# Attention and mixture-of-experts layer on one Trainium2 core: new places in the written-out order of the expert stage

## What is computed

```
x: (4, 512, 256), four batches of 512 tokens
mod = silu(c) @ wmod -> sa, ca, ga, sb, cb, gb per batch
h = layernorm(x) * (1 + ca) + sa
x = x + ga * attention(h)                       # 16 heads of 128, causal
h = layernorm(x) * (1 + cb) + sb
d = h @ down_w + down_b                         # 256 -> 128
probs = softmax(h @ router_w + router_b - cost); top 2 of 8; gate = softmax of the two
out = sum_k gate_k * sum_e expert_e(d * [e is chosen])     # hidden sizes 128 to 512, gelu
out = out + 0.1 * shared(d)
x = x + gb * (out @ up_w + up_b + gelu(h) @ core_w + core_b)
```

## Time and profile before

| | before |
|---|---|
| median of 3 runs | 822.38 us |
| the profiled execution | 828.41 us |
| its span (first to last instruction) | 826.3 us |
| TensorE busy | 794.3 us (96%) |
| VectorE busy | 680.8 us (82%) |
| ScalarE busy | 628.8 us (76%) |
| GpSimd busy | 439.7 us (53%) |

### The profile page before, as it was taken

How to read it: one execution, slowest core, us unless ns; L and a number is a source line. 1 busy time by engine, 2 the same in 40 slices (tenths; PEclk the granted TensorE clock), 3 DMA queues, 4 the chain that set the end, 5 groups by cost and what they waited for, 6 DMA issues and landing times.

```text
span 826.3 us, 14461 instructions
## 1 busy us (share of the span) xinstructions
PE 794.3 (96%) x4806; PEld 710.6 (86%) x4806; DVE 680.8 (82%) x1649; ACT 628.8 (76%) x1417; POOL 439.7 (53%) x305
## 2 busy tenths in 40 slices
PE   8899899999999999999999999999999898999897
PEld 7689888999999999999999999999988676777686
DVE  4789898888888888888888878889898987797766
ACT  3787878778878888778887788887779586675864
POOL 2555355654555556544566544575453474667544
PEclk8999999999999999999999999999999899999999
DMA  7253233343223433233233442244232141111131
GB/s 247 75 168 72 57 88 91 92 112 73 64 68 81 111 107 90 68 85 73 64 91 90 103 109 64 64 110 115 66 74 54 46 129 34 53 43 66 64 97 58
DMA packets 47593, 70.54 MB, mean 85 GB/s; under 512 B 5536, under 2 KB 38464, under 8 KB 47392
## 3 DMA queue, kind: packets, MB, share of 16 engines
q1 hardware_dynamic: 47008, 68.81, 31.7%
q0 software_dynamic: 368, 0.81, 0.3%
q10 hardware_dynamic: 144, 0.00, 0.0%
HBM read 25.49 MB, written 2.17 MB: 33 GB/s over the span
## 4 chain that ended last, share of the span: by engine, by line
PE 69%; ACT 16%; DVE 10%; issue 4%; DMA 1%; SPq 0%; DVEq 0%; ACTq 0%
PE M L729 10%; PE M L730 10%; PE M L728 10%; PE T L728 7%; PE T L729 7%; PE T L730 7%; PE S L728 5%; PE S L730 5%; PE S L729 5%; ACT PB L620 3%; ACT PB L669 3%; DVE S L1136 2%; ACT pth L696 2%; ACT qk L682 1%; DVE Gr L1294 1%
## 5 line engine op out<-in xcount | busy, mean ns | idle before, releaser
L620 ACT ACTIVATE PB<-S,nb 128x128 f32<-128x128 f32 (+3 forms) x256 | 133.9, 533 | 109.3 <-DVE nb L1136 109.3
L570 POOL TENSOR_TENSOR X<-X,fb 128x512 f32<-128x512 f32 x64 | 83.0, 1298 | 245.6 <-DVE fb L1173 245.6
L577 POOL TENSOR_TENSOR ptl<-ptl,pth 128x640 fp32r<-128x640 f32 x126 | 195.8, 1576 | 32.0 <-ACT pth L696 32.0
L669 ACT ACTIVATE PB<-PB,ri 128x256 f32<-128x256 f32 (+3 forms) x256 | 124.5, 581 | 6.8 <-DVE ri L1145 6.7
L1136 DVE CUSTOM_DVE_ANT_0 S<-S,cc 128x128 f32<-128x128 f32 (+3 forms) x256 | 117.5, 522 | 1.3 <-PE S L730 1.3
L1121 DVE TENSOR_TENSOR qk<-M,qk 128x512 fp32r<-128x512 f32 x108 | 74.6, 690 | 45.2 <-ACT qk L682 45.2
L1152 DVE STREAM_TRANSPOSE gab<-PB 128x256 f32<-128x256 f32 (+2 forms) x192 | 109.3, 622 | 0.0
L728 PE MATMUL S<-qk 128*128 128x128 f32 (+3 forms) x256 | 86.8, 339 | 4.7 <-DVE qk L1121 4.7
L728 PE MATMUL M<-hh,W 128*128 128x512 f32 x222 | 87.3, 393 | 0.7 <-DVE hl L1107 0.7
L696 ACT CAST pth<-ptl 128x640 fp32r<-128x640 f32 x128 | 87.9, 746 | 0.1
L730 PE MATMUL M<-hh,W 128*128 128x512 f32 x222 | 87.2, 393 | 0.0
(11 more groups left out here) (255 smaller groups left out, 2444.9 us busy)
## 6 DMA issues: line engine op xcount, KB each, us to landing
ptl<-gab SPq DMA_DIRECT2D x256, 160.0 KB, 3.1
stage<-in_wat SPq DMA_DIRECT2D x16, 512.0 KB, 5.0
gab<-scw SPq DMA_DIRECT2D x16, 256.0 KB, 3.3
tmp<-scw SPq DMA_DIRECT2D x16, 256.0 KB, 3.6
X<-in_x SPq DMA_DIRECT2D x3, 512.0 KB, 8.6
stage<-in_wfa SPq DMA_DIRECT2D x3, 512.0 KB, 4.8
out<-X SPq DMA_DIRECT2D x3, 512.0 KB, 2.9
X<-in_wmod SPq DMA_DIRECT2D x1, 1024.0 KB, 11.7
```

The lines of the kernel that those rows point to most:

```text
L570: pool.tensor_tensor(X[:, a:a + 512], X[:, a:a + 512], fb[:, c2 * 512:c2 * 512 + 512], ALU.add).then_inc(s_y, 1)
L577: pool.tensor_tensor(ptl[u % 2][:, s], ptl[u % 2][:, s].bitcast(F32), pth[u % 2][:, s].bitcast(F32), ALU.subtract).then_inc(s_pl, 1)
L620: ins = act.activation(PB[:, P_OFF[i]:P_OFF[i] + w], PS[bk][:, a:a + w], ACT.Exp, bias=nb[:, i:i + 1], scale=-1.0, accum_out=sm[:, i:i + 1])
L669: act.activation(p, p, ACT.Copy, scale=ri[:, i:i + 1]).then_inc(s_P3, 1)
```

## The change

All of it is in the order of the list, with one group of three VectorE instructions moved besides. No product, buffer or engine changes.

- Steps 3 to 9 of batch 0's router go from chunks 0:0 to 0:2 into the end of the attention, ahead of VectorE's part of `dn` 0. Steps 10 to 14 go from 0:4 and 0:5 to 0:0 and 0:1, its `wt` from 0:7 to 0:3, the last `pt` from 0:5 to 0:3, the last `z` from 0:7 to 0:6, the last two `wo` from 0:9 and 0:10 to 0:8 and 0:9, `wh` 21 and 22 one and two chunks earlier.
- The three instructions that clear `wgw` and `Dm` go from behind the low part of `z` 61 to ahead of step 10 of batch 0.
- Layernorm of batches 2 and 3: `nm` 6 in 0:10 and 0:11 (was 0:9, 0:10), `nm` 7 in 0:19 and 0:20 (was 0:18, 0:19), each at least a chunk behind its `nb`.
- Batch 1: steps 3 to 7 in 0:11 and 0:12 (were 0:12 and 0:13), `wt` in 0:19 (was 1:1); `dta` one chunk earlier for two of its three parts, `dt` in 1:0 (was 1:1).
- Batch 2: `r` in 1:5 (was 1:7), `wt` in 2:0 (was 2:2). Batch 3: `r` in 2:4 (was 2:1), steps 3 to 14 in 2:14 to 2:19 (were 2:8 to 2:13), `wt` in 3:0 (was 3:2).
- `gx` 0 in 1:7 and 1:9 (was 1:8, 1:10), its `hs` as much earlier; the second `gx` of batches 1, 2 and 3 one chunk later. `o` 0 in 1:6 (was 1:7). `up` of batches 1 and 2 in chunks 7 and 8 (were 8 and 10), of batch 0 in 1:11 and 1:12 (was 1:11 and 1:13). `xb` of batches 1 and 2 in chunk 0 of the next batch (was 19), of batch 3 in 3:16 (was 3:18).

```diff
--- before.py
+++ after.py
@@ -105,7 +105,8 @@
         plan += post.get(i, [])
     u = NU - 1
     plan += [("S", u), ("wo", u // 2 - 2, 1), ("v", u // 2, 1), ("ex", u), ("ri", u), ("r", 0), ("rs", 0, 1),
-             ("rs", 0, 2), ("pt", u - 1), ("ra",), ("wx", u // 2 - 2, 1), ("b1",), ("dn", 0), ("z", u - 2)]
+             ("rs", 0, 2), ("pt", u - 1), ("ra",), ("wx", u // 2 - 2, 1), ("b1",)] + [("rs", 0, k) for k in range(3, 10)] + [
+             ("dn", 0), ("z", u - 2)]
     return plan + [("norm", u), ("ty", u), ("tr", u), ("z", u - 1), ("ld", 22)]
 
 
@@ -117,57 +118,60 @@
     def put(t, j, *events):
         at.setdefault((t, j), []).extend(events)
 
-    put(0, 0, ("rs", 0, 3), ("rs", 0, 4), ("rs", 0, 5))
-    put(0, 1, ("wo", last - 1, 0), ("rs", 0, 6), ("rs", 0, 7))
-    put(0, 2, ("wo", last - 1, 1), ("rs", 0, 8), ("rs", 0, 9))
-    put(0, 3, ("wh", 21))
-    put(0, 4, ("rs", 0, 10), ("rs", 0, 11), ("rs", 0, 12))
-    put(0, 5, ("rs", 0, 13), ("rs", 0, 14), ("pt", NU - 1))
-    put(0, 6, ("wh", 22))
-    put(0, 7, ("wt", 0), ("wl", 0), ("wl", 1), ("wl", 2), ("z", NU - 1), ("st", 6, 0), ("st", 6, 1))
-    put(0, 8, ("st", 6, 2), ("st", 6, 3))
-    put(0, 9, ("wo", last, 0), ("nb", 6), ("nm", 6, 0))
-    put(0, 10, ("wo", last, 1), ("wl", 3), ("nm", 6, 1))
-    put(0, 11, ("d0", 0))
+    def router(b, steps, weights):
+
+        first, exps, rest = steps
+        put(*first, ("r", b))
+        put(first[0], first[1] + 1, ("rs", b, 1), ("rs", b, 2))
+        for c in range(4):
+            put(exps[0], exps[1] + c, ("rp", b, c))
+        for k, j in enumerate(rest[1], 3):
+            put(rest[0], j, ("rs", b, k))
+        put(*weights, ("wt", b))
+
+    put(0, 0, ("rs", 0, 10), ("rs", 0, 11), ("rs", 0, 12))
+    put(0, 1, ("wo", last - 1, 0), ("rs", 0, 13), ("rs", 0, 14))
+    put(0, 2, ("wo", last - 1, 1), ("wh", 21))
+    put(0, 3, ("pt", NU - 1), ("wt", 0), ("wl", 0), ("wl", 1), ("wl", 2))
+    put(0, 4, ("wh", 22))
+    router(1, ((0, 5), (0, 7), (0, (11, 11, 11, 12, 12, 14, 14, 16, 16, 16, 17, 17))), (0, 19))
+    put(0, 6, ("z", NU - 1))
+    put(0, 7, ("st", 6, 0), ("st", 6, 1))
+    put(0, 8, ("wo", last, 0), ("st", 6, 2), ("st", 6, 3))
+    put(0, 9, ("wo", last, 1), ("wl", 3), ("nb", 6))
+    put(0, 10, ("nm", 6, 0))
+    put(0, 11, ("nm", 6, 1), ("d0", 0))
     put(0, 12, ("d0", 1))
-    put(0, 13, ("dn", 1), ("d0", 2))
-    put(0, 14, ("h2", 2, 0))
-    put(0, 16, ("h2", 2, 1))
-    for k, j in enumerate((15, 16, 16, 17)):
-        put(0, j, ("st", 7, k))
-    put(0, 18, ("nb", 7), ("nm", 7, 0), ("dta", 0))
-    put(0, 19, ("nm", 7, 1), ("dta", 1))
-    put(0, 20, ("dta", 2))
-    put(1, 1, ("dt",), ("xb", 0))
-    put(1, 2, ("h2", 3, 0))
-    put(1, 4, ("h2", 3, 1))
-    put(1, 5, ("D", 0))
-    put(1, 6, ("hs", 0, 0))
-    put(1, 8, ("gx", 0, 0), ("hs", 0, 1))
-    put(1, 10, ("gx", 0, 1))
-    for b, n in ((1, 5), (2, 28), (3, 43)):
-        def at_(i, *events):
-            put(*divmod(i, NC + 1), *events)
-        at_(n, ("r", b))
-        at_(n + 1, ("rs", b, 1), ("rs", b, 2))
-        for c in range(4):
-            at_(n + 2 + c, ("rp", b, c))
-        for k, m in enumerate((7, 7, 7, 8, 8, 9, 9, 11, 11, 11, 12, 12), 3):
-            at_(n + m, ("rs", b, k))
-        at_((22, 44, 65)[b - 1], ("wt", b))
+    put(0, 13, ("dn", 1))
+    put(0, 14, ("h2", 2, 0), ("d0", 2))
+    put(0, 15, ("h2", 2, 1), ("st", 7, 0))
+    put(0, 16, ("st", 7, 1), ("st", 7, 2))
+    put(0, 17, ("st", 7, 3), ("dta", 0))
+    put(0, 18, ("nb", 7), ("dta", 1))
+    put(0, 19, ("nm", 7, 0), ("dta", 2))
+    put(0, 20, ("nm", 7, 1))
+    put(1, 0, ("dt",))
+    put(1, 3, ("h2", 3, 0))
+    put(1, 4, ("h2", 3, 1), ("D", 0))
+    put(1, 5, ("hs", 0, 0))
+    put(1, 7, ("gx", 0, 0), ("hs", 0, 1))
+    put(1, 9, ("gx", 0, 1))
+    late = 14, 14, 14, 15, 15, 16, 16, 18, 18, 18, 19, 19
+    router(2, ((1, 5), (1, 8), (1, late)), (2, 0))
+    router(3, ((2, 4), (2, 5), (2, late)), (3, 0))
     for t in range(1, B):
-        late = 3 * (t == 1)
+        first = t == 1
+        put(t, 0, ("xb", t - 1))
         put(t, 3, ("D", t))
-        put(t, 6 + late // 3, ("o", t - 1))
-        put(t, 8 + late, ("up", t - 1, 0))
-        put(t, 9 + late, ("hs", t, 0))
-        put(t, 10 + late, ("up", t - 1, 1))
-        put(t, 11 + late, ("gx", t, 0), ("hs", t, 1))
-        put(t, 13 + late, ("gx", t, 1))
+        put(t, 6, ("o", t - 1))
+        put(t, 11 if first else 7, ("up", t - 1, 0))
+        put(t, 12 if first else 8, ("up", t - 1, 1))
+        put(t, 12 if first else 9, ("hs", t, 0))
+        put(t, 14 if first else 11, ("gx", t, 0), ("hs", t, 1))
+        put(t, 17 if first else 14, ("gx", t, 1))
         if t + 1 < B:
             put(t, 17, ("dn", t + 1))
-            put(t, 19, ("xb", t))
-    put(B - 1, 18, ("xb", B - 1))
+    put(B - 1, 16, ("xb", B - 1))
     chunks = B * (NC + 1)
     plan, later = [], []
     for n in range(chunks + LAG + 1):
@@ -1119,10 +1123,6 @@
                         hi, lo = zs(ev[1])
                     src = bank(ev)[:].rearrange("p (s n) -> p s n", s=2) if kind == "z" else bank(ev)[:]
                     v.tensor_tensor(lo, src, hi.bitcast(F32), ALU.subtract).then_inc(me, 1)
-                    if ev == ("z", NU - 3):
-                        v.tensor_scalar(wgw[:, 0:384], cc[:, 0:384], 0.0, None, ALU.mult)
-                        v.tensor_scalar(Dm[:], cc[0:96, 0:128], 0.0, None, ALU.mult)
-                        link(v.tensor_copy(wgw[:, 384:512], ident))
                 elif kind == "S":
                     u = ev[1]
                     if u > 0:
@@ -1175,6 +1175,10 @@
                                     ALU.mult).then_inc(me, 1)
                 elif kind in ("r", "rs"):
                     b, k = ev[1], (0 if kind == "r" else ev[2])
+                    if (b, k) == (0, 10):
+                        v.tensor_scalar(wgw[:, 0:384], cc[:, 0:384], 0.0, None, ALU.mult)
+                        v.tensor_scalar(Dm[:], cc[0:96, 0:128], 0.0, None, ALU.mult)
+                        link(v.tensor_copy(wgw[:, 384:512], ident))
                     if k:
                         v.wait_ge(s_rt, 15 * b + k)
                     router(ev, b, k).then_inc(s_rt, 1)
```

## The result

The kernel after takes **819.08 us** (median of 12 executions, 817.11 to 820.94), the kernel before 824.17 on the same chip (12 executions, 819.92 to 828.21): a ratio of 0.9935, with a 95% interval of 0.9915 to 0.9956. A second measurement on another chip gave 819.37 against 822.83, 0.9954 (0.9930 to 0.9978). The change gains 3.5 to 5.1 us where 9.3 were forecast, and about 3.4 when all executions of both kernels are put together. The direction was right, the size was not.

The account below looks back on a forecast made before the run. TensorE's order was the bound, with 26.8 of the stage's 188.6 us lost to waits and slow clock. After, 12.7 of waits and 4.8 for three falls make 17.5, so 9.3 less: 822.4 to 813.1 us, range 808.3 to 820.3.

Parts of the forecast that it names:

- sum after: Whole expert stage: waits and small rests left after the change, 12.7 us, plus three clock falls, 4.8, make 17.5.
- the median of before lies 6.0 lower; I take the same difference from it: Final time: the 9.3 us gained on the profiled execution, 828.4, is taken from the median 822.4, giving 813.1.
- I take 1.6 us for one fall: Expert stage: each drop of TensorE's clock to 1.2 GHz costs 1.6 us, half of 3.4 less a little hidden.
- the sum of TensorE's idle time in 0:11 to 1:4 as before: Sign of being wrong, late batch 0 to early batch 1: TensorE's total idle time there stays unchanged.
- `wt` 0 in 0:3: Batch 0: TensorE waits 2.65 us for VectorE's step 14, held by GpSimd's first `wo` addition.
- 0:11 to 1:4 ... 4.9: Late batch 0 to early batch 1: 4.9 us of waits plus one clock fall, for 7.2 lost before.
- `gx` 0: 1:5 to 1:13: wait of 0.6 us for 1.82, no clock fall, since GpSimd's powers do not hold VectorE.
- 1:14 to 2:16: Late batch 1 through most of batch 2: 2.4 us of waits plus one clock fall, for 6.5 lost before.
- (b): Rival, stretches holding a `wt`: the wait only moves, 3.7 us less, 818.7 us; 22 in 100.
- (a): Rival, whole stage: the clock does not fall, 14.1 us less, 808.3 us; 12 in 100.
- (c): Rival, 2:16 and 3:16: the expert sums stay late, gain 6.9 us, 815.5 us; 12 in 100.
- (d): Rival, the four `wt`: they become the bound, waits double, six falls, 3.5 us slower, 825.9 us; 9 in 100.

Follow-up runs that it names:

- e7: Kernel after with `wt` 0 in 0:5, the last `z` in 0:8 and the last two `wo` in 0:10 and 0:11: 815.36 us, ratio to before 0.9913.
- e8: e7 with `wt` 1 in 1:0 and `wt` 2 in 2:1, one chunk later each: 815.47 us, ratio to before 0.9905.
- e11: e8 with `dn` 2 in 1:15 and not in 1:17: 815.95 us, ratio to before 0.9907.
- e1: Kernel before, unchanged, measured once more: 821.99 us, ratio to before 1.0006.
- e0: Kernel after, unchanged, measured once more on another chip: 819.37 us, ratio to before 0.9954.
- e6: Kernel after with `nm` 7 a chunk sooner, back in 0:18 and 0:19: 822.64 us, ratio to before 0.9999.
- e5: Kernel after with `xb` of batches 1 and 2 back in chunk 19: 825.50 us, ratio to before 1.0037.
- e2: Kernel after with `wt` 0 in 0:5 and not in 0:3: 821.76 us, ratio to before 0.9988.
- e9: Kernel after with the second `gx` of batch 1 back in 1:16: 820.73 us, ratio to before 0.9972.
- e10: Kernel after with the second `h2` transpose of batch 2 back in 0:16 from 0:15: 821.63 us, ratio to before 0.9982.
- e4: Kernel before with only the batch 0 part (router, `wt` 0, last `pt`, `z`, `wo`, `wh`, clearing): 825.88 us, ratio to before 1.0033.
- e12: Kernel after with the batch 0 part undone, all else of the change kept: 819.48 us, ratio to before 0.9951.

## Why the prediction was right in its direction and wrong in its size

**The larger step that failed: the "sum after", 12.7 with "small rests of 0.1 at seven places" for 0.7 of it, was set against 26.8.** The 26.8 of before is what is left of the stage's length when the needs are taken off, so it holds every loss, named or not. The 12.7 of after is built up from waits that I could name. Of the 9.3 that came out, 5.6 were waits (18.3, which is 26.8 less 8.5 for the clock, to 12.7) and 3.7 clock (8.5 to 4.8). Counted alike, the named waits in the stage go from 15.3 to 12.8, 2.5 less and not 5.6, and TensorE's idle time goes down by 2.6. The rest is in both kernels: after, at full clock, loses 18.1, and 18.1 - 12.8 = 5.3 of it stand in no row of these views. With the same needs e7, e8 and e11, which have no fall in the stage either, leave 5.4, 5.6 and 6.5. The prediction left 0.7 of this to the kernel after.

That the profiled execution came out at 819.17 where 819.1 was forecast is luck. The waits and rests were 5.4 too low (12.7 for 18.1), and three falls for 4.8 did not come in that execution: 17.5 for 18.1.

**The second step: "the median of before lies 6.0 lower; I take the same difference from it".** A median execution has less clock to give back than one with 17 us at half clock in the stage. Twice (1 - mean clock) times the span is the time at half clock: 33 us in the profiled execution of before, 18.5 in the mean of the 96, 12.3 in that of after's 22. How much of the 18.5 lies in the stage can only be estimated: with 3.4 to 13.6 in the first 100 us (e1) and some 2 in the last microseconds, 3 to 13 and not 17. Profile against profile, the clock is 6.1 of the 8.7 us of stage. Over all executions, 0.0038 of mean clock at 510 to 600 us is 1.9 to 2.3 us. At equal clock (0.989 to 0.991) 42 executions of before have a median of 822.0 and 7 of after 819.5; one step higher (0.992 to 0.994) it is 820.4 and 818.7: 1.7 to 2.5 that are not clock, and 1.5 by one common slope for all 118. Together that is about the 3.4 that all executions show. The second profiles of the two programs say much the same: e1's stage has 13.6 us at half clock and takes 185.9, e0's has 10.2 and takes 182.8, some 3 less. The right sum would have been some 2 for waits and 2 for the clock, from 822.4 to about 818.5. Putting only this second step right would have left 5.6 + 2 = 7.6, far from what was measured. That the clock itself gains is plausible by the waits that went, but that it gains in after because of them is only argued: e0 shows that the same waits may come with or without a fall.

**"I take 1.6 us for one fall":** 1.0 to 1.25 by the slopes of e1, and 1.2 between the profiles of before and after (6.1 us for 17.1 at half clock), with single pairs at 1.0 and 2.7.

**The prediction's own sign of being wrong came true:** "the sum of TensorE's idle time in 0:11 to 1:4 as before". It was 4.83 us (34.19 less 29.36 busy) and is 4.68 (33.52 less 28.84). Of the signs of being right, 1:5 starts at 696.7 and 2:17 at 763.4, as said, and no `dt` or `D` waits; but `wt` 1 waits 1.21 and not some 3, and the slow clock of the stage is 0 in after's first profile and 10.2 us in e0's, where about 10 was said.

**The waits after, place by place:** the total of the named ones is near (12.8 in the stage; 12.0 without the small rests), but not the terms.

- `wt` 0 in 0:3: 2.65 forecast, 2.70 measured, and its cause is as told. The timeline of all engines:

```profile
644.32 1.26 POOL L574 TENSOR_TENSOR X<-X,fb 128x512 f32<-128x512 f32 x1 [6.54 <-DVE fb L1173]
...
644.48 1.15 DVE L1015 TENSOR_TENSOR wg<-rt 128x32 f32<-128x32 f32 x1
```

The `wg` step that takes 0.19 in batch 2 takes 1.15 under GpSimd's addition. "`pt` 63 leaves GpSimd 0.4 before `z` wants it" came down to 0.1 (652.6 to 652.7), since GpSimd's second addition took 2.21 us and not 1.3. Of the gap between 4.3 lost here and 3.4, 0.6 is in the needs: `z` takes 1.96 of TensorE (652.74 to 654.70) and not 1.4. "A fall of the clock" here came in e0's profile and not in after's.

- "0:11 to 1:4 ... 4.9": 6.5 lost. The late sum in 0:16 (1.4 forecast) did not come, nor did the 3.2 at `wt` 1 (1.21) or the 0.3 at `dt`. The walk left out the banks: `h2` of batch 2 in 0:15 takes the bank of `dn` 1's product and waits 1.31 for its low part, `dta` waits 1.46 for the low part of `h2` itself, and two more waits for banks take 0.70 in 1:4 and, just behind this stretch, 0.41 in 1:5. I had followed VectorE's queue with TensorE's main operands and not with the tiles that `h2`, `dta` and `dn` pass on. One backlog of VectorE, met at other doors: 4.7 us of waits where 4.9 were forecast, at other places and as long as before.

- `nm` 7: "no longer blocks ScalarE for 5.07 us", right; the idle time before it is 1.90 us in after, and TensorE doesn't meet it. e6 shows what it is worth.

- `gx` 0: 0.6 forecast by rows, 1.4 by the rule of the Trainium skill that the prediction names, 0.72 measured. The timeline of all engines shows why:

```profile
708.92 0.81 DVE L1291 TENSOR_TENSOR gxl<-stage,gxh 128x512 fp32r<-128x512 f32 x1
709.13 2.10 POOL L556 TENSOR_TENSOR rt<-ebase,rt 128x8 f32<-128x8 f32 x1
```

VectorE's subtraction with two SBUF inputs ends 1.5 us before GpSimd's power does. The power doesn't hold it. It had begun 0.21 us before the power, but in the earlier trace rows the same instruction begins inside a power and takes 0.69 us all the same. The Trainium skill (GPSIMD Engine Reference, Specifications) has the SBUF interfaces contended by any VectorE instruction with two SBUF inputs; here the trace agrees for GpSimd's additions (1.15 us for the `wg` step above) and not for its powers.

- 1:14 to 2:16: 2.4 of waits and a fall forecast, 5.0 lost, no fall. `up` waits 0.38 and 0.39 (0.5 forecast). `wt` 2 waits 1.20 (1.9), `D` not at all. Left out: **the first product of batch 2 needs the low part of `dn` 2**, and that stands on VectorE behind the held `gx` 1. Timeline of all engines:

```profile
728.39 1.27 POOL L547 TENSOR_TENSOR stage<-stage,prod 128x512 f32<-128x512 f32 x1
728.46 1.74 DVE L1291 TENSOR_TENSOR gxl<-stage,gxh 128x512 fp32r<-128x512 f32 x1
...
730.13 0.68 DVE L1284 TENSOR_TENSOR ur<-M,ur 128x512 fp32r<-128x512 f32 x1
```

The prediction had "perhaps a hold ahead of the steps" and charged it to `wt` 2 alone; TensorE met it sooner, with 2.09 us at 2:0's first product.

- `xb`: "2.1 us of hold gone", right and undersold: e5 puts the place of `xb` at about 6 us, since both `wt` that moved sooner hang on it.

**The rivals.** (b), *the wait only moves*, at 818.7, came nearest, and its reason holds for much of the stage: e2, e9, e10 and e11 each took away a wait and found most of it a few chunks later, and e8 found one of its two. It said no change in the three stretches with a `wt`; in fact the large waits went and others came, and some 2 us stayed gone. The other argument in it, that the busiest engine leaves an order nothing to win, doesn't hold: TensorE is 96% busy in e7 too, which is 4 us faster than after. (a), no fall at all, is what after's profile shows, but at 819.2 and not at 808.3: the rests that the sum left out stand in the place of the falls. (c) did not come; the sums wait 0.2. (d) did not come for after, but e5 shows that its mechanism is real: held in these very steps, `wt` costs more than the change gains.

**What stays open.** How often a wait of 1.5 to 3 us brings a fall is known only from the few profiled executions (e0); over all executions only the mean clock of the whole span stands here. What the 5.3 us of unnamed rest consist of was not looked into. Which parts of the change bring the gain on top of before was tested, e4 and e12 aside, by undoing single steps; the new places of batch 3's router, of `up`, of `o` and of `gx` 0 were not undone. Nor was it tried whether a lighter VectorE queue in 0:12 to 1:4 would let e8's order gain in full.

The best version that was run is e7, with e8 and e11 equal to it within the measurement: 0.991 of before, some 4 us better than after.

## What to carry to other kernels

Count the losses after the change as the losses before it were counted: a remainder (length less needs) is only to be set against a remainder, and a list of named waits against a list. And before subtracting a difference of profiles from a median, split it into waits and clock: twice (1 - mean clock) times the span says how much slow clock the profiled execution holds, and an execution 6 us above the median may hold much of the gain one is about to promise. In a queue that is in order, a wait moved off one instruction is paid at the next that hangs on the same engine's backlog; it is won only where the late producer can be given the time as well (e7: `wt`, `z` and `wo` moved together) or loses work or a hold (`xb`, `nm`). When a move is walked through, list every reader of every buffer and bank that passes by there, the first product of the next batch among them.

## What the runs showed that was not expected

GpSimd's addition on 512 columns takes 1.26 to 1.30 us, but 2.21 when VectorE runs a subtraction on 1024 columns from SBUF beside it. The holding works in both directions, and it was this second one that used up the slack of `pt` 63 (2.22 in e2 and in e7, beside the same subtraction). The timeline of all engines of after:

```profile
647.20 1.22 DVE L1057 TENSOR_TENSOR W<-stage,W 128x1024 fp32r<-128x1024 f32 x1
647.37 2.21 POOL L574 TENSOR_TENSOR X<-X,fb 128x512 f32<-128x512 f32 x1 [1.78 <-DVE fb L1173]
```

A VectorE instruction with one SBUF input on four columns was held as well (1.94 us in e5). And the time of one and the same program follows the granted clock closely enough (-0.90 over 96 executions, 817.63 us at 0.998, 828.16 at 0.980) that the clock of the profiled execution should be read before its length is.
